# Attention values in query rows: V as the moving operand, the softmax sum as a column, and a transposition behind it

## The reference

```python
B, S, HID = (1, 256, 256)
H, KVH, HD = (32, 8, 64)
q, k = apply_rope(q), apply_rope(k)
k = jnp.repeat(k, groups, axis=1)          # groups = 4
v = jnp.repeat(v, groups, axis=1)
logits = jnp.einsum('bhqd,bhkd->bhqk', q, k) * scale
logits = jnp.where(causal, logits, jnp.finfo(dtype).min)
attn = jax.nn.softmax(logits, axis=-1)
out = jnp.einsum('bhqk,bhkd->bhqd', attn, v)
out = out.transpose(0, 2, 1, 3).reshape(b, s, H * HD)
return out @ Wo.T
```

## Time and profile before

| | us |
|---|---|
| median of 3 runs | 427.15 (425.34 to 429.74) |
| the profiled execution's own time | 427.22 |
| its span, first to last instruction | 425.4 |
| PE, PEld busy | 386.0, 310.8 |
| DVE, ACT, POOL busy | 351.5, 269.8, 132.8 |
| mean granted TensorE clock | 0.976 of full speed |

### The profile page before, as it was taken

How to read it: one execution, slowest core, us unless ns; L and a number is a source line. 1 busy time by engine, 2 the same in 40 slices (tenths; PEclk the granted TensorE clock), 3 DMA queues, 4 the chain that set the end, 5 groups by cost and what they waited for, 6 DMA issues and landing times.

```text
span 425.4 us, 7535 instructions
## 1 busy us (share of the span) xinstructions
PE 386.0 (91%) x2605; PEld 310.8 (73%) x2636; DVE 351.5 (83%) x479; ACT 269.8 (63%) x775; POOL 132.8 (31%) x163
## 2 busy tenths in 40 slices
PE   4989997999999799988997999889597999599996
PEld 2735875888788688867886788678486887488885
DVE  1885857998999999999999999999979997475532
ACT  2468798677877577758775777587466668433221
POOL 2522521262245233523452335244422241020000
PEclk9999999999999989999999899999978999989999
DMA  9862483376858296669482965594766632200000
GB/s 230 168 116 51 102 239 91 101 210 139 241 114 217 51 238 183 159 183 220 111 214 51 243 178 124 149 218 115 189 173 115 183 76 49 51 0 26 25 27 25
DMA packets 51702, 57.39 MB, mean 135 GB/s; under 512 B 29753, under 2 KB 41281, under 8 KB 51665
## 3 DMA queue, kind: packets, MB, share of 16 engines
q0 software_dynamic: 7136, 23.01, 26.3%
q10 hardware_dynamic: 12464, 22.97, 16.3%
q1 hardware_dynamic: 32064, 10.94, 12.6%
HBM read 26.36 MB, written 1.18 MB: 65 GB/s over the span
## 4 chain that ended last, share of the span: by engine, by line
PE 62%; DVE 17%; ACT 10%; issue 7%; DMA 2%; POOL 1%; ACTq 0%; DVEq 0%
PE ps_p L1081 16%; PE ps_so L1099 7%; PE ps_p L1203 7%; PE ps_r L1153 6%; PE ps_so L1183 5%; PE ps_p L1312 5%; PE ps_so L1295 5%; ACT prob L452 4%; DVE state L827 3%; DVE state L820 2%; PE ps_so L1187 2%; ACT pt L458 2%; DVE nmax L740 2%; DVE state L833 2%; PE ps_r L1164 2%
## 5 line engine op out<-in xcount | busy, mean ns | idle before, releaser
L452 ACT ACTIVATE prob<-ps_so,nmax 128x256 f32<-128x256 f32 (+1 forms) x256 | 104.8, 443 | 43.6 <-DVE nmax L740 43.6
L375 POOL TENSOR_TENSOR rc<-rc,rs 128x512 f32<-128x512 f32 x39 | 55.5, 1422 | 89.6 <-DVE rs L728 71.4
L827 DVE TENSOR_TENSOR_SCAN state<-decay,state 128x1024 f32<-128x1024 f32 x32 | 79.0, 2470 | 1.1
L458 ACT ACTIVATE pt<-ps_r 128x512 f32<-128x512 f32 x96 | 53.7, 593 | 22.8 <-PE ps_r L1153 22.3
L740 DVE TENSOR_REDUCE nmax<-ps_so 128x2 f32<-128x512 f32 (+1 forms) x96 | 60.2, 683 | 8.7 <-PE ps_so L1110 8.6
L1081 PE MATMUL ps_p<-xt_all,wq 128*128 128x256 f32 x256 | 66.6, 405 | 0.3 <-ACT sin_s L578 0.3
L382 POOL DMA_DIRECT2D y<-state x32 | 29.3, 914 | 114.9 <-DVE state L833 114.9
L1203 PE MATMUL ps_p<-wo,attn_t 128*128 128x256 f32 x256 | 61.8, 387 | 0.2 <-DVE attn_t L843 0.2
L452 ACT ACTIVATION_READ_ACCUMULATOR prob<-ps_so,nmax 128x1 f32 x256 | 58.5, 229 | 0.0
L1081 PEld LDWEIGHTS ps_p<-xt_all,wq 128*128 128x128 f32 x256 | 48.2, 198 | 13.3 <-issue 6.5
L1153 PE MATMUL ps_r<-ident,prob 128*128 128x128 f32 x384 | 53.1, 275 | 3.5 <-ACT pt L458 1.7
(11 more groups left out here) (118 smaller groups left out, 523.0 us busy)
## 6 DMA issues: line engine op xcount, KB each, us to landing
bc<-bc_scratch ACTq DMA_DIRECT2D x32, 512.0 KB, 5.7
y<-state POOLq DMA_DIRECT2D x32, 512.0 KB, 5.4
qt<-rc SPq DMA_DIRECT2D x32, 128.0 KB, 3.1
qt<-rc POOLq DMA_DIRECT2D x32, 128.0 KB, 3.1
wq<-wqkv_t SPq DMA_DIRECT2D x32, 64.0 KB, 2.8
wo<-wo_t ACTq DMA_DIRECT2D x8, 256.0 KB, 4.5
kt<-rc SPq DMA_DIRECT2D x28, 64.0 KB, 3.7
kt<-rc POOLq DMA_DIRECT2D x28, 64.0 KB, 3.3
```

The source lines that it names most:

```text
L375: nc.gpsimd.tensor_tensor(o, o, s, ALU.add).then_inc(rope_add, 1)
L452: nc.scalar.activation(o, i, ACT.Exp, bias=nmax[:, r, c:c + 1], accum_out=rsum[:, r, GRP + head:GRP + head + 1]).then_inc(exp_done, 1)
L458: nc.scalar.activation(pt[:, fill, :], ps_r[:, fill % 2, :], ACT.Copy).then_inc(pt_copied, 1)
L827: nc.vector.tensor_tensor_scan(state[:, v % 2, :], decay[:, v % 2, :], state[:, v % 2, :], 0.0, ALU.mult, ALU.add).then_inc(decay_free, 1)
```

## The change

values(u) becomes pt stationary (128 keys by 128 queries) and V moving (64 columns): 8 matmuls with the first 128 keys, then 4 with the second, which only the later queries need. The result stands in query rows: the row sum is a value of the partition, and scale_attn multiplies ps_o by rinv, broadcast over the 64 columns of each head, into rep_s. PE's transpose_attn(u) brings that into the layout of attn_t in four pieces, into ps_r bank 1 (unit 31: ps_p bank 0), and ScalarE's copy_attn(u) copies it to attn_t. widen, replicate and copy_rep are gone with the two widened buffers. transpose_attn(u-1) stands in PE's unit u where replicate(u) stood, copy_attn(u-1) where copy_rep(u) stood. values(u) now waits for the third copy of pt only before its last 4 matmuls. reciprocals(u) moves on VectorE from behind the scan of unit u-1 to behind negmax(u+1) of unit u. attn_t is complete one unit later, so the last pairs of projections move: unit 30 has pair 4 alone, pair 5 stands in unit 31 where pair 6 stood, pair 6 behind values(31).

```diff
@@ module @@
-WO_PAIRS.update({UNITS - 4 + i: ((B - 1, 2 * i), (B - 1, 2 * i + 1)) for i in range(3)})
+WO_PAIRS.update({UNITS - 4 + i: ((B - 1, 2 * i), (B - 1, 2 * i + 1)) for i in range(2)})
+WO_PAIRS[UNITS - 2] = ((B - 1, 4),)
...
+        attn_bank = lambda u: ps_r[:, 1, :] if u < UNITS - 1 else ps_p[:, 0, :]
@@ scalar @@
-            def widen(u):
-            def copy_rep(u):
...
+            def copy_attn(u):
+
+                b, g = divmod(u, KVH)
+                act.wait_ge(attn_ps, u + 1)
+                if b:
+                    act.wait_ge(wo_done, u - KVH + 1)
+                nc.scalar.activation(attn_t[:, 2 * g:2 * g + 2, :],
+                                     attn_bank(u).rearrange("p (k s) -> p k s", k=2), ACT.Copy
+                                     ).then_inc(attn_copied, 1)
...
                 copy_pt(u, 2)
-                copy_rep(u)
+                if u:
+                    copy_attn(u - 1)
...
                 load_next_bc(u)
-                if nxt:
-                    widen(u + 1)
...
             silu_z(1)
+            copy_attn(UNITS - 1)
             copy_x2t(0)
@@ vector @@
             def scale_attn(u):
 
-                b, g = divmod(u, KVH)
                 dve.wait_ge(pv_done, u + 1)
-                dve.wait_ge(rep_copied, u + 1)
-                if b:
-                    dve.wait_ge(wo_done, u - KVH + 1)
-                nc.vector.tensor_tensor(attn_t[:, 2 * g:2 * g + 2, :], ps_o[:].rearrange("p (k s) -> p k s", k=2),
-                                        rep_s[:, u % 2, :].rearrange("p (k s) -> p k s", k=2), ALU.mult
-                                        ).then_inc(attn_copied, 1)
+                dve.wait_ge(rinv_done, u + 1)
...
+                if u >= 2:
+                    dve.wait_ge(attn_ps, u - 1)
+                nc.vector.tensor_tensor(rep_s[:, u % 2, :].rearrange("p (c d) -> p c d", d=HD),
+                                        ps_o[:].rearrange("p (c d) -> p c d", d=HD),
+                                        rinv[:, u % 2, :].rearrange("p (c k) -> p c k", k=1).to_broadcast(
+                                            [P, 2 * GRP, HD]), ALU.mult).then_inc(attn_scaled, 1)
...
                     negmax(u + 1)
+                reciprocals(u)
...
-                if u + 1 < UNITS:
-                    reciprocals(u + 1)
                 for v in todo[:1]:
                     times_c(v)
...
             norm_x2(0)
+            reciprocals(UNITS - 1)
             scale_attn(UNITS - 1)
@@ tensor @@
                 elif fill == 1:
-                    if u:
-                        pe.wait_ge(rep_copied, u)
+                    if u >= 2:
+                        pe.wait_ge(attn_copied, u - 1)
...
-            def replicate(u):
...
+            def transpose_attn(u):
+
+                pe.wait_ge(attn_scaled, u + 1)
+                if u + 1 < UNITS:
+                    pe.wait_ge(pt_copied, (u + 1) * 3 + 2)
+                else:
+                    pe.wait_ge(rope_mul, 2 * len(ROPES))
                 for pair in range(GRP // 2):
                     for t in range(TB):
...
+                        last = nc.tensor.transpose(attn_bank(u)[:, pair * S + t * P:pair * S + (t + 1) * P],
+                                                   rep_s[:, u % 2, t * S + pair * P:t * S + (pair + 1) * P], ident[:])
+                last.then_inc(attn_ps, 1)
 
             def values(u):
 
                 slot, i = (u // KG) % 2, u % KG
                 if u:
-                    pe.wait_ge(attn_copied, u)
+                    pe.wait_ge(attn_scaled, u)
...
+                pe.wait_ge(pt_copied, u * 3 + 2)
+                v = [vv[:, slot, part, i * HD:(i + 1) * HD] for part in range(2)]
+                for h in range(GRP):
+                    for t in range(TB):
+                        nc.tensor.matmul(ps_o[:, t * S + h * HD:t * S + (h + 1) * HD],
+                                         pt[:, h // 2, h % 2 * S + t * P:h % 2 * S + (t + 1) * P], v[0],
+                                         start=(h == 0 and t == 0), stop=False)
                 pe.wait_ge(pt_copied, u * 3 + 3)
-                for pair in range(GRP // 2):
-                    for part in range(2):
-                        for odd in range(2):
...
+                for h in range(GRP):
+                    last = nc.tensor.matmul(ps_o[:, S + h * HD:S + (h + 1) * HD], pt[:, 2, h * P:(h + 1) * P], v[1],
+                                            start=False, stop=(h == GRP - 1))
                 last.then_inc(pv_done, 1)
...
                 transpose_p(u, 2)
-                replicate(u)
+                if u:
+                    transpose_attn(u - 1)
...
             transpose_p(UNITS - 1, 1)
-            out_project((LAST, 6))
+            out_project((LAST, 5))
             transpose_p(UNITS - 1, 2)
-            replicate(UNITS - 1)
+            transpose_attn(UNITS - 2)
             transpose_gz(0)
             values(UNITS - 1)
+            out_project((LAST, 6))
+            transpose_attn(UNITS - 1)
             transpose_x2(0)
             transpose_gz(1)
             out_project((LAST, KVH - 1))
```

More of the change, by code:

```diff
@@ L237, in decoder_layer @@
         rope_add = sem("rope_add")
-        wide_done, rep_done, rep_copied = sem("wide_done"), sem("rep_done"), sem("rep_copied")
+        attn_scaled, attn_ps = sem("attn_scaled"), sem("attn_ps")
         decay_done = sem("decay_done")
@@ L590, in _ @@
                                      ).then_inc(xdbl_sb, 1)
-            widen(0)
             nc.scalar.activation(a_exp[:], par[:, :, DC + 3:], ACT.Exp).then_inc(a_done, 1)
@@ L782, in _ @@
             ln_apply(1, B, 2)
-            reciprocals(0)
             def prepare_scan(g):
@@ L836, in scale_attn @@
             def scale_attn(u):
-                b, g = divmod(u, KVH)
                 dve.wait_ge(pv_done, u + 1)
-                dve.wait_ge(rep_copied, u + 1)
-                if b:
-                    dve.wait_ge(wo_done, u - KVH + 1)
-                nc.vector.tensor_tensor(attn_t[:, 2 * g:2 * g + 2, :], ps_o[:].rearrange("p (k s) -> p k s", k=2),
-                                        rep_s[:, u % 2, :].rearrange("p (k s) -> p k s", k=2), ALU.mult
-                                        ).then_inc(attn_copied, 1)
+                dve.wait_ge(rinv_done, u + 1)
+                if u == 0:
+                    dve.wait_ge(k_first[0], 16)
+                    dve.wait_ge(k_first[1], 16)
+                    dve.wait_ge(k_sp[0], k_due(0))
+                    dve.wait_ge(k_pool[0], k_due(0))
+                if u >= 2:
[4 more added lines that the diff above has]
+                                            [P, 2 * GRP, HD]), ALU.mult).then_inc(attn_scaled, 1)
             def add_attention(b):
@@ L1154, in transpose_p @@
                 last.then_inc(pt_done, 1)
-            def replicate(u):
-                pe.wait_ge(wide_done, u + 1)
-                pe.wait_ge(pt_copied, u * 3 + 2)
+            def transpose_attn(u):
[4 more added lines that the diff above has]
+                    pe.wait_ge(rope_mul, 2 * len(ROPES))
                 for pair in range(GRP // 2):
                     for t in range(TB):
-                        c = t * GRP + 2 * pair
-                        src = rwide(u)[:, c:c + 2, :].rearrange("p o k -> p (o k)")
-                        last = nc.tensor.transpose(ps_r[:, 1, pair * S + t * P:pair * S + (t + 1) * P],
-                                                   src, ident[:])
-                last.then_inc(rep_done, 1)
+                        last = nc.tensor.transpose(attn_bank(u)[:, pair * S + t * P:pair * S + (t + 1) * P],
+                                                   rep_s[:, u % 2, t * S + pair * P:t * S + (pair + 1) * P], ident[:])
+                last.then_inc(attn_ps, 1)
             def values(u):
@@ L1175, in values @@
                 pe.wait_ge(v_copied, u // KG + 1)
-                pe.wait_ge(pt_copied, u * 3 + 3)
-                for pair in range(GRP // 2):
-                    for part in range(2):
-                        for odd in range(2):
-                            o = ps_o[odd * HD:(odd + 1) * HD, :]
-                            v = vv[:, slot, part, i * HD:(i + 1) * HD]
-                            if part == 0:
-                                last = nc.tensor.matmul(o[:, pair * S:(pair + 1) * S], v,
-                                                        pt[:, pair, odd * S:(odd + 1) * S], start=True, stop=False)
-                            else:
-                                h = 2 * pair + odd
-                                last = nc.tensor.matmul(o[:, pair * S + P:(pair + 1) * S], v,
-                                                        pt[:, 2, h * P:(h + 1) * P], start=False, stop=True)
+                pe.wait_ge(pt_copied, u * 3 + 2)
[5 more added lines that the diff above has]
+                                         start=(h == 0 and t == 0), stop=False)
+                pe.wait_ge(pt_copied, u * 3 + 3)
```

(5 more changed lines are left out.)

20 lines of the change are left out of this document (removed).

## The result

| | before | after |
|---|---|---|
| median | 428.23 (4 runs, 425.34 to 429.74) | 444.61 (4 runs, 443.69 to 444.94) |
| the profiled execution, its span | 427.22, 425.4 | 444.41, 442.6 |
| PE, PEld busy | 386.0, 310.8 | 417.2, 364.8 |
| DVE, ACT, POOL busy | 351.5, 269.8, 132.8 | 353.8, 249.6, 132.5 |
| mean granted TensorE clock | 0.976 | 0.985 |

After takes 1.0387 times as long as before, with a 95% interval of 1.0325 to 1.045. (One more run of before joined the three that were known.) The forecast was 438.5 in a range of 428 to 449: the direction and the main mechanism are right, the size is 6 us short, and two steps of the sum, the tail above all, were wrong.

A forecast was written before the change was run, and what follows sets the result against it. PE was taken to set the pace in 21 of 31 units, with VectorE or ScalarE waits in the others. 18.8 - 0.2 - 2.5 - 2.4 - 1.0 - 1.1 - 0.3 = +11.3 gave 438.5 us, range 428 to 449.

The forecast's parts named there:

- the tail: End of the kernel: values(31) and eight projection matmuls go into PE's idle time, the last projection ends slightly earlier; -0.3 us.
- The load as the price of values: PE in values(): 24 loads of 128 columns, 0.108 us each, hide the matmuls; values 2.70 us, a unit +0.94.
- the 20 places: Values and intervals where PE sets the pace: 20 x 0.94 = +18.8 us, less 0.2 of a wait.
- rivals of 0.079: Loads in values() start 0.079 us apart, as the scores' loads do: unit +0.25, total 422, faster; chance 0.09.
- wholly hidden loads: Loads in values() overlap wholly, 0.054 us a pair: unit -0.33, total 409; chance 0.05.
- load plus matmul: Load and matmul in values() run in turn, 0.162 us a pair: unit +2.2, total 472; chance 0.05.
- interval 2: End of values(2) to end of values(3): without widen ScalarE's third copy of pt comes earlier, 8.8 for 11.3; -2.5 us.
- The price of the broadcast factor: VectorE's scale_attn: it keeps its size, and a broadcast factor should cost the same.
- The double-scan units: Intervals after units 10, 14, 18, 22: transpose_attn waits 1.1 us, clock kept; -2.4 us for 10 and 18, -1.0 for 14 and 22.
- new-stalls rival: transpose_attn waits 2.9 us for VectorE after the four double-scan units and the clock falls: 451; chance 0.11.
- Units 25 to 28: From values(25) to values(28): the V fill's wait stays, the 2.67 wait for exponentials goes; -1.1 us.
- then 0.8 of wait for scale_attn(27): Within units 25 to 28: PE waits 0.8 us for scale_attn(27), and 0.94 is added.

The follow-up runs named there:

- e1: The changed kernel with 128 columns of V streamed behind each load of values() instead of 64; 440.41 us, ratio to before 1.0309.
- e3: The changed kernel with values() loading only the first 64 of each block's 128 queries as weights; 422.5 us, ratio to before 0.989.
- e8: The kernel before with only the reciprocals moved to where after has them, and widen along with them; 420.5 us, ratio to before 0.985.
- e2: The changed kernel with only 32 of V's 64 columns streamed in each matmul of values(); 445.68 us, ratio to before 1.0433.
- e6: The changed kernel with values(u) waiting for all three copies of pt before its first matmul; 450.55 us, ratio to before 1.0563.
- e7: The changed kernel with values(31) ahead of transpose_gz(0) and transpose_x2(0) ahead of transpose_attn(31), ScalarE's copies likewise; 440.94 us, ratio to before 1.0319.
- e4: The changed kernel with each 128-query block split into two of 64 columns, one per column half of the array, complete result; 422.33 us, ratio to before 0.9877.
- e5: The changed kernel with the reciprocals put back between scan and times_c, where they stood before; 447.32 us, ratio to before 1.0489.

## Why the prediction was right, and where it fell short

**The load as the price of values: right.** A step of 0.108 was taken from the first two loads of a query fill, 0.112 was measured, and e1 to e3 show that it is the load alone. 23 steps of 0.004 more give 0.09, and a plain unit grew by 1.03 for 0.94. Over the 20 places that is 1.1 net, since values(0) itself came only 0.48 later. This is a mis-sized term, not a wrong one. The row gave 0.11 to two digits; the forecast's own bound of 0.114 a pair covered it. The rivals of 0.079, of wholly hidden loads and of load plus matmul are all refuted by the eight loads at 0.111.

**ScalarE and VectorE: right.** ScalarE lost 20 us of busy time, and what shows of it is interval 2, -2.6 for -2.5. Behind the double scans e8, which keeps widen, has 11.07 where after has 11.01. The price of the broadcast factor was nothing: scale_attn lasts 0.68 in both the earlier trace rows.

**The double-scan units: right to 0.1.** The transposes of rep_s wait 1.09, forecast 1.1, and the clock stays up as assumed. The new-stalls rival (2.9 us in those four units, 451) did not occur there.

**Units 25 to 28: wrong in size, -0.1 for -1.1.** The step "then 0.8 of wait for scale_attn(27)" failed. In the trace of after this wait is 2.92 and the clock falls behind it. PEld's and VectorE's timelines:

```profile
334.67 0.42 PEld L1154 LDWEIGHTS ps_r<-ident,rep_s 128*128 128x128 f32 x4 [2.92 <-DVE rep_s L831]
335.06 3.05 PEld L1191 LDWEIGHTS ps_p<-wo,attn_t 128*128 128x128 f32 x8
```
```profile
328.01 1.22 DVE L804 TENSOR_TENSOR state<-du,bc 128x1024 f32<-128x1024 f32 x1 [1.27 <-DMA y<-state]
```

VectorE's drive waits 1.27 for a transfer of y, which I had not counted, and the loads of one projection take 3.05 for 1.60. The price that the stall rival foretold was paid here, once: 2.1 more of wait than forecast and 1.45 more of loads. Against it stands the V fill one unit earlier, whose wait I had left as it was. PEld's timelines of it, after and then e2:

```profile
319.63 1.59 PEld L1070 LDWEIGHTS ps_p<-wv,xt_all 128*128 128x128 f32 x8 [3.41 <-DVE rs L715]
```
```profile
323.75 3.06 PEld L1070 LDWEIGHTS ps_p<-wv,xt_all 128*128 128x128 f32 x8 [3.42 <-DVE rs L715]
```

In after it waits 3.41 for before's 4.45, and its loads last 1.59 where before they lasted 3.06. In e2 and e6, whose units are as long as after's, they last 3.06 as in before, and the 2.92 of wait does not follow. The three intervals from values(25) are 17.84, 10.28, 12.33 and 17.96, 9.96, 12.20 there, against 14.96, 14.51, 11.66 in after: 40.5 and 40.1 against 41.1, with the forecast at 40.2. e7 is as after (fill 1.59, then a wait of 3.85; 41.9). So PE loses the time at one place or at the other, and the sum moves by 2 us at most (39.8 in e1 to 41.9 in e7). The transfer of y alone does not decide which: in e1 and e2 the drive waits for it too (0.91 and 1.54) without the wait of 2.92. What decides it is open.

**The tail: the step that failed, +3.4 for -0.3.** I put "values(31) and eight projection matmuls go into that idle time". They do not: they stand behind transpose_gz(0) and its wait. With unit 30 eight projection loads shorter PE comes there 2.97 us before the gated y (2.28 in before, where the clock held), and the clock falls in front of 24 loads instead of 16 and a projection more. The x2 transposes come 389.75 - 379.67 = 10.1 us behind the first gz transposes, where in before it was 370.22 - 365.74 = 4.5 with an idle time of 2.62 in it: the work that I meant to put into that idle time overran it. I had priced the last projection at full and at half clock but not values(31) and pair 6, which is where it counted. e7 recovers it by the order of the queue alone.

**The sum.** 1.1 + 0.2 + 1.0 + 3.7, less 0.1 at interval 2, account for the 5.9 between +11.3 and the 17.2 of the profiled executions, and the medians differ by 16.4.

## What to carry to other kernels

Before swapping stationary and moving operands of small matmuls, count the columns loaded in each unit and whether both halves of the array are used: here 24 f32 loads of 128 columns cost 2.78 us where 16, or 48, of 64 columns cost 1.45 to 1.55. Relief for an engine that waits most of the time is worth nothing, while moving one small operation that stood behind a semaphore between two long scans was worth 1.5% (0.7 to 2.3). And in the order of a queue, put work that is ready in front of the wait that comes last, above all where the clock may fall behind that wait.

## What was not expected of the hardware

- Two column halves of the array take f32 loads side by side: 48 loads of 64 columns last 1.55 us (e4), as 24 do (e3).
- 128 moving columns hide behind a 128-column f32 load as wholly as 32 do: units of 9.93 in e1, e2 and after.
- The clock can make a wait count double: one of 2.97 in the tail was followed by 5.1 us for 2.8 and 3.1 for 1.6 (after). Yet waits of 1.09 in four other units, of 2.03 in e4 and of 2.28 in before's tail were followed by loads at full speed.
- Executions of nearly the same program differ at the start: in e2, e6 and e7 the profiled one has half clock from values(0) on and loses 3 to 4 us before values(1), in after, e1 and e5 it does not.
